# Self-attention scores on the two halves of the rows, with one unpadded copy of the turned keys

## The chip, the cores and the metric

The kernel runs on one core of a Trainium2 chip. The metric is the device time of one execution in microseconds (us), as the median of the runs made.

## The reference

One decoder layer over x of shape (4, 512, 256), in float32: causal linear self-attention with a quadratic feature map, cross-attention over a context of 1601 tokens, a mixture of eight experts (two for each token), each followed by a residual and a layer norm. The change lies in the self-attention:

```python
q = (x @ Wq.T)  # 16 heads of 16 features; k and v likewise
def feature_map(x):             # after a layer norm over the 16 features
    xn = norm(x) * gamma + beta
    diag, off = xn * xn, xn[..., IU] * xn[..., JU]
    return concat([diag * 16 ** -0.5, off * (2 / 16) ** 0.5])
kv_cum = cumsum(phi_k[..., :, None] * v[..., None, :], axis=time)
num = einsum('bhtf,bhtfd->bhtd', phi_q, kv_cum)
den = einsum('bhtf,bhtf->bht', phi_q, cumsum(phi_k)) + EPS
x = layernorm(x + (num / den) @ Wo.T)
```

The inner product of two such feature vectors is (q.k / 4) squared. The kernel therefore computes for each head the scores k.q, squares them, sets those of later keys to zero and multiplies them with the values and a column of ones.

## The kernel before

**Stages.** The opening loads and splits weights and prepares batch 0. Then comes the self-attention of four batches, then cross-attention, then the experts. Every engine runs its own program; semaphores order them.

**Numbers.** Float32 operands of a product are split into a high part in fp32r and the rest. A head has 16 features; q and k are laid out so that a head takes 64 rows (16 features in four slots: high, high, low, low for q and high, low, high, low for k in QX and KX), which makes the sum over 64 rows the sum over the four split products. Two heads fill the 128 rows.

**Quads and slots.** The 16 heads are taken in four quads of four (g), and the 512 keys in four blocks of 128 (c). A slot n is one quad and one block, n = 4g + c, 16 slots in a batch. In a slot the four heads j = 0 to 3 each have one score product (`score`, L1577; matmul L1584) of 128 keys against the queries from that block on: 512, 384, 256 or 128 columns for c = 0 to 3.

**Turned keys and queries.** `turn` on TensorE (L1562) transposes two heads at a time (q = 0, 1 within a quad) into bank 0 for the queries and bank 1 for the keys. ACT copies the queries whole into qT (L801): rows 0 to 63 hold the even head, rows 64 to 127 the odd one. DVE copies the keys in two casts of 64 rows (L1086, L1087) into kT, which has one plane of 128 rows for each of the four heads; the other 64 rows of each plane were set to zero by two memsets in the opening (L1027, L1028). So the score of a head contracts over all 128 rows, and the zeros cut the other head of the pair. TensorE may not turn the next keys before kT_ok says that bank 1 was read, and the first score of a quad waits for both turns.

**The order in a slot.** On TensorE (`attention`, L1641) slot n has: scores 0 and 1 of slot n + 1; the first half of the slot's other steps; scores 2 and 3; the four value products of slot n (`value`, L1594, 32 output rows for each head, with a different 32 columns of the array); the second half of the other steps. The scores use banks 3, 4 and 5 in turn, so a score waits until ACT has squared the third before it (`sqr_ok`, L1583). ACT squares (L836), POOL masks the diagonal block (L620), the values wait for the mask.

**The other steps** are written out in `alongside(n, b)` (L459). In slots 0 to 5 the batch before is finished (back, yt, out, stats); in slots 0 to 8 the next batch is projected and its features are made ("project qk" L1539, "project v" L1550, squares, variance, normalise L1073, affine on POOL L601 and L603); the turns of quad g + 1 stand at the end of quad g - 1 and the start of quad g, those of quad 3 in slots 7 and 8; slots 13 to 15 turn the first quads of the next batch. Slots 9 to 12 have hardly any such step on TensorE. On DVE the turns stand behind the features of the same slot. SP loads the turned input of the next batch but one once its buffer is free (L529), ACT splits it (L762), in slot 12 the one for two batches later.

Between the opening and the loop ACT issues nine copies that fill a DRAM buffer for the experts, XG, with numbers (L856, L859).

## Time and profile before

| | us |
|---|---|
| median of 3 runs | 1341.96 (1336.73 to 1345.72) |
| profiled execution | 1343.06 |
| its span, first to last instruction | 1341.3 |
| opening, ahead of the first score | 0 to 57 |
| self-attention loop | 57 to 282 |
| cross-attention and experts | about 300 to the end |

| over the span | busy us | share |
|---|---|---|
| TensorE, matmuls | 1188.4 | 89% |
| VectorE (DVE) | 745.2 | 56% |
| ScalarE (ACT) | 593.6 | 44% |
| GpSimd (POOL) | 700.1 | 52% |

All score products of the self-attention (L1584) take 76.5 us of matmul time, and the 64 casts of the turned keys (L1086, L1087) 43.9 us of DVE. Times in the trace count from the start of the span. A busy share of a matmul is no measure of its pace, since its end is modelled and successive ones overlap; the distance from one start to the next is.

### The profile page before, as it was taken

How to read it: one execution, taken by the hardware profiler on the slowest of the kernel's cores; microseconds unless marked ns; L12 is line 12 of the kernel's file. 1: busy time of each engine (PE TensorE's matmuls, PEld its weight loads, DVE VectorE, ACT ScalarE, POOL GpSimd, SP SyncE). 2: the span in 40 equal slices, each digit the busy share in tenths (PEclk: the TensorE clock that was granted, in tenths of full speed). 3: DMA queues.
4: the chain of work that ended last, by engine and by line, in shares of the span. 5: the costliest groups of instructions: out<-in, count | busy, mean ns of one | idle time of the engine just before them, and what ended most of it. 6: DMA issues, size and time to landing. Idle time of an engine off the chain costs nothing.

```text
span 1341.3 us, 19028 instructions
## 1 busy us (share of the span) xinstructions
PE 1188.4 (89%) x6456; PEld 696.4 (52%) x6456; DVE 745.2 (56%) x1364; ACT 593.6 (44%) x1033; POOL 700.1 (52%) x621
## 2 busy tenths in 40 slices
PE   4388898856999999999999999999999899999990
PEld 3254565533555545555555555555555356666660
DVE  5655857547236664555684467654657754433325
ACT  3366756632444464344644435643544423222222
POOL 1354737331358776577787577695777221311112
PEclk9599998886899999999999999999999999999995
DMA  5492000010000010000110000000001831211105
GB/s 170 148 327 90 2 1 1 1 50 26 0 0 1 1 50 1 1 1 0 35 32 17 1 1 1 25 32 1 1 1 62 281 115 44 76 42 39 45 24 188
DMA packets 33133, 64.84 MB, mean 48 GB/s; under 512 B 4349, under 2 KB 22526, under 8 KB 32768
## 3 DMA queue, kind: packets, MB, share of 16 engines
q1 hardware_dynamic: 23328, 32.41, 7.6%
q10 hardware_dynamic: 6304, 22.76, 5.4%
q0 software_dynamic: 3408, 8.46, 1.8%
q8 instruction: 54, 0.88, 0.3%
q14 instruction: 39, 0.32, 0.1%
HBM read 53.06 MB, written 28.51 MB: 61 GB/s over the span
## 4 chain that ended last, share of the span: by engine, by line
PE 71%; DVE 13%; issue 5%; ACT 5%; DMA 4%; ACTq 1%; POOL 1%; SPq 0%; POOLq 0%; DVEq 0%
PE PS L1772 15%; PE PS L1783 12%; PE PS L1675 10%; PE PS L1840 9%; DVE mxp L1405 5%; PE PS L1858 5%; DMA xt_raw<-in_xt 3%; PE PS L1688 3%; PE PS L1594 2%; PE PS L229 2%; PE PS L1573 2%; PE PS L1584 2%; PE PS L230 2%; PE PS L231 2%; PE PS L1849 1%
## 5 line engine op out<-in xcount | busy, mean ns | idle before, releaser
L682 POOL TENSOR_TENSOR acc<-acc,PX 128x1024 f32<-128x1024 f32 (+1 forms) x165 | 392.6, 2379 | 127.5 <-ACT PX L955 118.3
L955 ACT ACTIVATE PX<-PS 128x1024 f32<-128x1024 f32 (+1 forms) x208 | 212.3, 1025 | 257.7 <-PE PS L1772 254.5
L1405 DVE TENSOR_REDUCE mxp<-PS 128x2 f32<-128x804 f32 x256 | 242.1, 990 | 123.5 <-PE PS L1688 122.6
L1783 PE MATMUL PS<-PX,V 128*64 128x512 f32 (+1 forms) x832 | 207.8, 609 | 0.2 <-ACT PX L955 0.2
L1840 PE MATMUL PS<-W,XBT 128*128 x312 | 147.1, 595 | 1.1 <-ACT XBT L987 0.8
L731 POOL DMA_INDIRECT Y<-yb,goal_u x39 | 38.3, 982 | 202.5 <-DVE yb L1487 196.5
L620 POOL TENSOR_SCALAR_AFFINE_SELECT A<-A 128x128 f32<-128x128 f32 x256 | 85.8, 350 | 105.8 <-ACT A L836 103.0
L836 ACT ACTIVATE A<-PS 128x512 f32<-128x512 f32 (+3 forms) x256 | 97.1, 447 | 64.8 <-PE PS L1584 58.3
L1772 PE MATMUL PS<-QH,KH 64*128 64x512 f32 (+1 forms) x416 | 102.8, 491 | 3.4 <-ACT PX L955 2.7
L1772 PEld LDWEIGHTS PS<-QH,KH 64*128 64x128 f32 (+1 forms) x416 | 38.3, 181 | 116.0 <-issue 79.7
L1584 PE MATMUL PS<-qT,kT 128*128 128x512 f32 (+3 forms) x256 | 76.5, 376 | 15.9 <-ACT A L836 10.7
L1783 PEld LDWEIGHTS PS<-PX,V 128*64 128x64 f32 (+1 forms) x832 | 48.4, 136 | 78.0 <-issue 72.3
L1772 PE MATMUL PS<-QH,KL 64*128 64x512 f32 (+1 forms) x416 | 82.8, 393 | 0.0
L1772 PE MATMUL PS<-MR,one_row 64*128 64x512 f32 (+1 forms) x416 | 82.7, 392 | 0.0
L1772 PE MATMUL PS<-QL,KH 64*128 64x512 f32 (+1 forms) x416 | 82.5, 393 | 0.0
L1224 DVE RECIPROCAL TR<-TR 128x256 f32<-128x256 f32 x32 | 55.8, 1746 | 47.2 <-ACT TR L930 47.2
L1688 PE MATMUL PS<-KH,QH 64*128 64x402 f32 x512 | 72.5, 356 | 5.8 <-DVE mxp L1405 5.8
L1840 PEld LDWEIGHTS PS<-W,XBT 128*128 128x128 f32 x312 | 55.9, 191 | 41.8 <-issue 40.2
L1858 PE MATMUL PS<-W,hT 128*128 x312 | 73.9, 380 | 0.8 <-ACT hT L1000 0.8
L994 ACT ACTIVATE gl<-PS 128x512 f32<-128x512 f32 x39 | 23.3, 597 | 114.3 <-PE PS L1840 114.3
L924 ACT COPY V<-PS 128x512 f32<-128x512 f32 (+1 forms) x52 | 30.5, 586 | 96.8 <-PE PS L1675 96.8
L679 POOL TENSOR_TENSOR acc<-PX 128x1024 f32<-128x1024 f32 x15 | 35.5, 2367 | 65.1 <-ACT PX L955 65.0
(278 smaller groups left out, 2153.5 us busy)
## 6 DMA issues: line engine op xcount, KB each, us to landing
W<-in_w SPq DMA_DIRECT2D x24, 512.0 KB, 5.3
XB<-XG ACTq DMA_DIRECT2D x39, 130.0 KB, 2.1
yl<-Y SPq DMA_DIRECT2D x8, 512.0 KB, 6.8
X<-in_x SPq DMA_DIRECT2D x1, 2048.0 KB, 11.8
out<-X SPq DMA_DIRECT2D x8, 256.0 KB, 2.1
xt_raw<-in_xt SPq DMA_DIRECT2D x3, 512.0 KB, 4.3
c_raw<-in_ctxt SPq DMA_DIRECT2D x6, 200.0 KB, 2.5
c_raw<-in_ctxt SPq DMA_DIRECT2D x12, 100.0 KB, 2.6
```

The lines of the kernel that those rows point to most:

```text
L620: pool.affine_select(out=blk, in_=blk, compare_op=ALU.is_ge, fill=0.0, base=0, pattern=[[1, P]], channel_multiplier=-1).then_inc(mask_ok, 1)
L682: ins = pool.tensor_tensor(sums[0:r], sums[0:r], PX[0:r, (NL * p + t) % NP, :, :], ALU.add)
L836: act.activation(A[:, u % 8, P * c:T], PS[:, score_bank(b, u), P * c:T], ACT.Square, scale=0.25).then_inc(sqr_ok, 1)
L955: act.activation(PX[0:r, u % NP, :, :], PS[0:r, score_buffer(u):score_buffer(u) + 2, :], ACT.Exp, scale=XD ** -0.5)\
L1405: dve.tensor_reduce(mxp[:, p % 2, :, v % NT, v // NT:v // NT + 1].rearrange("p a o -> p (a o)"), PS[:, k:k + 2, 0:BW], AX, ALU.max)\
L1584: pe.matmul(PS[:, score_bank(b, u), P * c:T], kT[:, g % 2, j, P * c:P * c + P], qT[:, g % 2, j // 2, P * c:T], start=True, stop=True).then ...
L1675: mm = pe.matmul(o, l, r, start=(n == 0), stop=(n == len(ops) - 1))
L1688: mm = pe.matmul(bank(bk + half, BW), QH[rows, p % 2, P * i:P * i + P], KH[rows, p % 2, BSTART[k]:BSTART[k] + BW], start=True, stop=True)
L1772: mm = pe.matmul(bank(score_buffer(u) + half, rows=r), lhs, q_[rows, p % 2, :], start=(n == 0), stop=(n == 3))
L1783: mm = pe.matmul(PS[rows, 4, :], V[0:LROWS[j], j, P * p + XD * half:P * p + XD * half + XD], PX[0:LROWS[j], u % NP, half, :], start=(j == ...
L1840: mm = pe.matmul(bank(2 * m + j % 2), XBT[:, j % 2, c, :], W13[:, bass.ds(e, 1), m, c, :].rearrange("p o n -> p (o n)"), start=(c == 0), s ...
L1858: mm = pe.matmul(bank(6, D), hT[:, j % 2, f, :], W2[:, bass.ds(e, 1), f, :].rearrange("p o n -> p (o n)"), start=(f == 0), stop=(f == FC - 1))
```

## The change

The turned keys get the layout of the turned queries: kT shrinks from four planes to two, and one cast of 128 rows replaces two of 64 rows. The memsets go. Each score product contracts over the 64 rows that hold its head, rows 0 to 63 for heads 0 and 2 and rows 64 to 127 for heads 1 and 3, in kT as in qT. kT_ok counts one for each turn instead of two, const_dve one instead of three. The three banks of the scores, the order of the steps and all other waits stay as they are.

```diff
--- before.py
+++ after.py
@@ -97,7 +97,7 @@
         QX = ss("QX", [P, NT, SH, 4, SF], f32r)
         KX = ss("KX", [P, NT, SH, 4, SF], f32r)
         qT = ss("qT", [P, 2, 2, T], f32r)
-        kT = ss("kT", [P, 2, 4, T], f32r)
+        kT = ss("kT", [P, 2, 2, T], f32r)
         A = ss("A", [P, 8, T])
         VS = ss("VS", [P, NT, SH, 2 * SF])
         osb = ss("osb", [P, 2, T])
@@ -1024,8 +1024,6 @@
         @block.vector
         def _(dve):
             dve.memset(VS[:, :, :, SF:], 1.0).then_inc(const_dve, 1)
-            dve.memset(as32(kT[64:P, :, 0:4:2, :]), 0.0).then_inc(const_dve, 1)
-            dve.memset(as32(kT[0:64, :, 1:4:2, :]), 0.0).then_inc(const_dve, 1)
             groups = [raw[:, c, 0:2 * D].rearrange("p (g f) -> p g f", f=SF) for c in range(KC)]
             dve.wait_ge(ld_q, 16)
             for c in range(KC):
@@ -1083,8 +1081,7 @@
 
             def turn(b, g, q):
                 dve.wait_ge(tk_mm, 8 * b + 2 * g + q + 1)
-                dve.tensor_copy(kT[0:64, g % 2, 2 * q, :], bank(1, rows=64)).then_inc(kT_ok, 1)
-                dve.tensor_copy(kT[64:P, g % 2, 2 * q + 1, :], PS[64:P, 1, :]).then_inc(kT_ok, 1)
+                dve.tensor_copy(kT[:, g % 2, q, :], bank(1)).then_inc(kT_ok, 1)
 
             def quad_out(b, g):
                 dve.wait_ge(av_mm, 16 * b + 4 * g + 4)
@@ -1533,7 +1530,7 @@
         @block.tensor
         def _(pe):
             pe.wait_ge(const_pool, 3)
-            pe.wait_ge(const_dve, 3)
+            pe.wait_ge(const_dve, 1)
             pe.wait_ge(w_lo, 1)
 
             def project_qk(t, i):
@@ -1576,13 +1573,14 @@
 
             def score(b, n, j):
                 g, c, u = n // NT, n % NT, 4 * n + j
+                rows = slice(64 * (j % 2), 64 * (j % 2) + 64)
                 if c == 0 and j == 0:
                     pe.wait_ge(qT_ok, 8 * b + 2 * g + 2)
-                    pe.wait_ge(kT_ok, 16 * b + 4 * g + 4)
+                    pe.wait_ge(kT_ok, 8 * b + 2 * g + 2)
                 if started(b, u, 3):
                     pe.wait_ge(sqr_ok, 64 * b + u - 2)
-                pe.matmul(PS[:, score_bank(b, u), P * c:T], kT[:, g % 2, j, P * c:P * c + P],
-                          qT[:, g % 2, j // 2, P * c:T], start=True, stop=True).then_inc(sc_mm, 1)
+                pe.matmul(PS[:, score_bank(b, u), P * c:T], kT[rows, g % 2, j // 2, P * c:P * c + P],
+                          qT[rows, g % 2, j // 2, P * c:T], start=True, stop=True).then_inc(sc_mm, 1)
 
             def value(b, n, j):
                 g, c, u = n // NT, n % NT, 4 * n + j
@@ -1615,7 +1613,7 @@
                 if kind == "turn q":
                     turn(b, s[1], s[2], QX, 0, tq_mm, qT_ok, 1)
                 if kind == "turn k":
-                    turn(b, s[1], s[2], KX, 1, tk_mm, kT_ok, 2)
+                    turn(b, s[1], s[2], KX, 1, tk_mm, kT_ok, 1)
                 if kind == "back":
                     back(b, i)
                 if kind == "yt":
```

## Rows read from the trace of the kernel before

**Rows 1.** Windows, all engines: window, length, busy (xcount) by engine, PEclk, DMA share, GB/s.

```profile
110.00:170.00 60.00, 50.42 (x350) 31.94 (x348) 42.65 (x91) 41.02 (x104) 33.87 (x73) 0.97 0.03 10
```

**Rows 2.** Chain (start, length, what), then timeline: start, us, engine, line, xcount [idle <-releaser].

```profile
65.86 44.31 DMA xt_raw<-in_xt
...
110.19 1.04 ACT L762 CAST xt_h<-xt_raw 128x1024 fp32r<-128x1024 f32 x1 [1.66 <-DMA xt_raw<-in_xt]
```

**Rows 3.** Tiles osb and kT: ns min/median/max, starts, forms; what readers waited for.

```profile
L1093 DVE COPY osb<-PS x16: 679/692/693, 77.6 to 282.8; 128x512 f32<-128x512 f32 x16
...
L1087 DVE CAST kT<-PS x32: 694/694/695, 52.7 to 270.5; 64x512 fp32r<-64x512 f32 x32
...
  ACT A L836: 35.6, 51
```

**Rows 4.** Timeline of the opening, and one DMA issue (KB, us to landing).

```profile
0.79 0.45 SPq L511 DMA_DIRECT2D raw<-in_wqkv  x1
...
4.71 1.76 DVE L1028 MEMSET kT<- 64x2048 f32 x1 [0.48 <-issue]
6.48 1.28 DVE L1032 TENSOR_REDUCE w_mean<-raw 128x32 f32<-128x512 f32 x2
...
53.50 1.09 PE L1573 MATMUL PS<-ident,KX 128*128 128x128 f32 x4 [0.64 <-DVE kT L1087]
...
raw<-in_wqkv SPq DMA_DIRECT2D x1, 768.0 KB, 5.7
```

**Rows 5.** Timeline at the start of batch 1's scores.

```profile
116.48 0.69 DVE L1087 CAST kT<-PS 64x512 fp32r<-64x512 f32 x1
...
117.28 0.70 PE L1584 MATMUL PS<-qT,kT 128*128 128x512 f32 x2 [1.55 <-issue]
```

**Rows 6.** Timeline of DVE, POOL, PE, slots 8 to 12 of batch 1.

```profile
156.03 0.69 DVE L1087 CAST kT<-PS 64x512 fp32r<-64x512 f32 x1
...
162.49 1.64 POOL L601 TENSOR_TENSOR feat<-feat,gam 128x512 f32<-128x512 f32 x1 [1.32 <-DVE feat L1073]
...
166.33 3.33 PE L1594 MATMUL PS<-A,VS 128*32 128x512 f32 x8 [1.94 <-POOL A L620]
```

**Rows 7.** Chain in batch 3: start, length, what.

```profile
268.31 0.71 DVE kT L1087
```

**Rows 8.** Timeline of PE in cross-attention, where shapes change.

```profile
576.48 0.40 PE L1772 MATMUL PS<-QH,KL 64*128 64x512 f32 x2
576.71 0.40 PE L1772 MATMUL PS<-MR,one_row 64*128 64x512 f32 x2
577.04 0.50 PE L229 MATMUL PS<-x_h,WQh 128*128 128x512 f32 x1
577.38 0.40 PE L230 MATMUL PS<-x_l,WQh 128*128 128x512 f32 x1
577.61 0.39 PE L231 MATMUL PS<-x_h,WQl 128*128 128x512 f32 x1
...
644.14 0.28 PE L230 MATMUL PS<-WOl,OHL 128*128 128x256 f32 x1
644.26 0.28 PE L231 MATMUL PS<-WOh,OHL 128*128 128x256 f32 x1
644.47 0.50 PE L1772 MATMUL PS<-QH,KH 64*128 64x512 f32 x2
644.81 0.39 PE L1772 MATMUL PS<-QL,KH 64*128 64x512 f32 x2
```

**Rows 9.** Timeline of PE in self-attention: scores before a projection.

```profile
135.25 0.60 PE L1584 MATMUL PS<-qT,kT 128*128 128x384 f32 x2
135.69 0.28 PE L229 MATMUL PS<-WSh,y_h 128*128 128x256 f32 x1
...
140.91 0.39 PE L1584 MATMUL PS<-qT,kT 128*128 128x256 f32 x2
141.14 0.28 PE L229 MATMUL PS<-WSh,y_h 128*128 128x256 f32 x1
```

## What the change will do to the time

> **What bounds the kernel now.** I read the busy time by stage first. In the self-attention stage no engine is full: of 60 us the TensorE records hold 50.4, DVE 42.7, ACT 41.0, POOL 33.9, at a granted clock of 0.97 [rows 1]. So the chain of work, not a busy share, has to say what an edit is worth. The change touches nothing but this stage (57 to 282 us) and the opening ahead of it.
>
> The chain shows a pin. The load of the third batch's turned input is issued at 65.86 us behind the copies that fill XG and lands at 110.17, 44.31 us later; ACT stands still for it 1.66 us (L762) [rows 2]. Whatever the score loop gains before 110 us in batch 0 is therefore waited away, except a gain in the opening, which starts the copies themselves earlier. So I count the opening, the last slots of batch 0 and batches 1 to 3.
>
> From there to 282 us a batch has two halves. In slots 0 to 8 and 13 to 15 TensorE has projections, transposes and output products between the scores and is nearly back to back; in slots 9 to 12 it has almost only scores and values and waits for squares (ACT), masks (POOL) and, through POOL's affine step, for DVE.
>
> **Part 1: the copies and memsets on DVE.** The 32 pairs of casts into kT (0.69 us each) become 32 casts of 128x512 [rows 3]. The nearest row for such a copy out of PSUM, osb of 128x512, takes 0.69 us as well [rows 3], so each turn loses 0.70 us, 22 us of DVE time in all. Where is it on the path?
>
> - Opening: the transposes of the second k turn wait for the L1087 cast (start 53.50, idle 0.64 for it) [rows 4], and the q turn behind them is what ACT copies before it issues the XG copies. 0.7 us, which moves the pin too.
> - The two memsets end at 4.71 + 1.76 = 6.47 us and the first reduce starts at 6.48; but the qkv weights, issued at 0.79 us, need 5.7 us, so they land at 6.5 anyway [rows 4]. Nothing; at most the 0.5 us that separates DVE instructions there. Without the DMA's cover it would be some 4 us.
> - Start of a batch: TensorE idles 1.55 us before its scores at 117.28, until the L1087 cast of 116.48 is done [rows 5]. The pattern stands three times (batches 1, 2, 3), all other engines idle too: 3 x 0.7 = 2.1 us.
> - Slots 7 to 11: DVE runs without a gap over two turns (the last cast at 156.03), the layer norm and the features; POOL waits 1.32 us for it at 162.49, then does its two affine steps (the first takes 1.64) and the masks, and the values at 166.33 have waited 1.94 us for a mask [rows 6]. Two casts less (1.4 us) put this about 1.3 us earlier, just what POOL idled; ACT's squares are late next. In batches 1 and 2: 2.7 us. In batch 0 the pin takes it, batch 3 has no features.
> - Batch 3: one turn has its cast on the chain at 268.31, the transposes behind it start at its end [rows 7]: 0.7 us.
>
> Sum of part 1: 0.7 + 2.1 + 2.7 + 0.7 = 6.2 us gained. The lower end is 2.8 (opening and batch starts alone, if another engine takes over elsewhere), the upper 7.
>
> **Part 2: the scores on half the rows.** A 512-column matmul over 128 rows takes 0.23 us from start to start (577.38 to 577.61), and a pair over 64 rows each, one per half, takes the same 0.23 (576.48 to 576.71) [rows 8]. So scores 0 and 1, and 2 and 3, of a slot can share one stream: per pair 0.23, 0.175, 0.12 and at most 0.09 us saved at 512, 384, 256 and 128 columns (from 0.23 for two of 256 [rows 9]).
>
> Against that stands the change of shape. In cross-attention the last pair of 64 rows before a 128-row product takes 0.33 instead of 0.23 (576.71 to 577.04) and that product 0.34 instead of 0.23; the other way 0.21 instead of 0.12 (644.26 to 644.47) and 0.34 instead of 0.23 [rows 8]. One boundary between the two shapes costs 0.20 us. Today scores and projections have one shape: two scores of 256 columns go straight into a projection in 0.23 [rows 9]. Where transposes stand ahead, 0.09 is paid already (0.44 for two of 384, not 0.35 [rows 9]), so such a boundary adds 0.11. The boundary between scores and values (128x32) exists now and stays. Afterwards a slot with other work reads: work, boundary, pair, boundary, work, boundary, pair, values. Three new boundaries for two pairs.
>
> The ledger of a full batch, what is paid minus what is saved, in us: slot 0: 0.42 - 0.35; 1: 0.51 - 0.24; 2: 0.20 - 0.05 (the rest lies under a wait for y_l); 3: nothing, since ACT's copy and squares time it; 4: 0.42 - 0.35; 5: 0.60 - 0.24; 6: 0.60 - 0.10; 7: 0.11 - 0.23; 8: 0.11 - 0.18; 9 to 12: nothing, since two shapes alternate now too and ACT and POOL time them; 13: 0.31 - 0.24; 14: 0.42 - 0.10; 15: 0.31 - 0.34. Together 4.0 paid and 2.4 saved, 1.6 us lost. Batches 1 and 2: 3.2. Slots 13 to 15 of batch 0: 1.0 - 0.7 = 0.3. Batch 3, which has fewer steps: 2.2 - 1.6 = 0.6. Sum of part 2: 11.2 paid, 7.1 saved, 4.1 us lost.
>
> The three banks are in both kernels: the fourth score of a slot waits for the first square, and scores idled 35.6 us for squares in all [rows 3]. This is why slots 3 and 9 to 12 give nothing: a score that starts sooner waits longer for ACT. The waits before a score are as before; kT_ok only counts half.
>
> The rows put a price of 0.20 us on a change of shape. The Trainium skill, TensorEngine Tiling (Array Packing), Key Properties, says that changing the tiling mode drains TensorE, which speaks against mixing 64-row scores into 128-row work; the trace agrees (0.20 us a boundary) and the sum goes by the trace. The same page, Theoretical Speedup, gives up to 2x for 64 rows; by that alone part 2 would be the gain of the first rival below.
>
> **Sum.** 4.1 - 6.2 = -2.1 us. The profiled execution took 1343.06 us with a span of 1341.3, so 1.8 lie around it; changed it would take 1341.0. It lies 1.1 us above the median 1341.96, so the forecast for the median is 1340.0, a change of 0.15%, which a comparison will hardly show.
>
> **Rivals.**
> 1. Shape changes cost nothing here, because each score waits for its own semaphore anyway. Then 7.1 + 6.2 = 13.3 us are gained: 1328.7. For it: pairs do run together in cross-attention. Against it: each boundary in rows 8 is paid, without exception. Chance 0.1.
> 2. Slower: the pairs don't overlap, because here each matmul has its own wait and its own increment where cross-attention increments once after a row of them. The boundaries remain: 11.2 - 6.2 = +5.0, so 1347.0. It decides for slower as soon as less than 5 of the 7.1 us are saved (6.2 + saving < 11.2). By the same mechanism 1% slower needs boundaries of 0.35 us. The drain that the page names is this rival's other half. Chance 0.2.
> 3. The DVE casts give only the lower 2.8 us, because ACT takes over in slots 8 to 12. Then 4.1 - 2.8 = +1.3: 1343.3. Chance 0.15.
> 4. Nothing in slots changes because the clock moves: TensorE falls to a lower granted clock after idle stretches, and a shifted idle stretch moves a few us either way. I give it 0.05 with no time of its own.
> The forecast has 0.5.
>
> **How the numbers follow.** The likeliest case is 1340, by itself 1335 to 1345 (half the boundaries' price either way, 2 us, and the spread of the runs shown, 1336.7 to 1345.7). The range reaches up to rival 2 with some spread, 1349, and down most of the way to rival 1, 1331. What a measurement of this kernel can tell from no change is about 1%, 13.4 us: faster means under 1328.5, slower over 1355.4. Only part of rival 1 gets under the first (0.05), and rival 2 with dearer boundaries over the second (0.04).
>
> **What would show it.** Right: one cast of about 0.69 us in each k turn; the idle before the first scores of batches 1 to 3 at 0.85 instead of 1.55 us; the 1.32 us that POOL waits for the features gone or ACT's; two scores of 256 columns in 0.12 to 0.2 us, and a 64-row pair ahead of a projection followed by a gap of 0.1 on either side; the stage's end (the last scores, now at 281 us) near 279; the load of the third input landing near 109.5. Wrong: pairs whose starts lie a full stream apart (rival 2), projections right behind scores with no gap (rival 1), an end of the stage over 285 or under 272, or times after it that differ in length, which would be no work of this change.

## The result, and the profile after

The changed kernel took 1353.34 us in the median of five runs (1349.41 to 1354.15), against 1344.75 us for the kernel before in runs beside it. The ratio is 1.0067, with an interval of 1.0045 to 1.009. Twelve more runs of it later gave 1351.56 us and 1.0051 (1.003 to 1.0071). So the change costs 7 to 9 us. I had forecast a gain of 2.

The profiled execution took 1352.12 us with a span of 1350.4. From its page come the sums by engine, the granted clock in 40 slices, and the group of the scores (busy us, mean ns, idle before them and what ended it); the last line is the clock of the kernel before:

```profile
PE 1202.1 (89%) x6456; PEld 685.6 (51%) x6456; DVE 717.2 (53%) x1330; ACT 594.6 (44%) x1033; POOL 700.0 (52%) x621
...
PEclk9599899876899999999999999999999999999995
...
L1582 PE MATMUL PS<-qT,kT 64*128 64x512 f32 (+3 forms) x256 | 64.1, 440 | 14.3 <-ACT A L836 11.7
...
PEclk9599998886899999999999999999999999999995
```

DVE is down by 28.0 us (745.2 to 717.2), of which the copies into kT are 21.9 and the memsets 3.5, and the score products by 12.4 us (76.5 to 64.1). Yet TensorE as a whole is busy 13.7 us *longer*. That can't be the scores; other products of the stage became longer. The clock slices are where to look: the fifth (135 to 169 us) and the ninth (270 to 304) are lower than before, the seventh is higher.

The last row of value products of the self-attention starts at 286.78 us, where it was at 281.41 before. A second profile of the changed kernel has it at 285.06. Behind that row the changed kernel needs another 1063.6 and 1061.8 us, the one before 1059.9, with the same instructions; so 2 to 4 us of the loss appear behind the stage.

### Where the changed kernel did what I said

The tile kT: ns min/median/max, first and last start, shapes.

```profile
L1582 PE MATMUL PS<-qT,kT x256: 276/436/794, 53.9 to 286.4; 64*128 64x512 f32 x32, 64*128 64x384 f32 x32, 64*128 64x256 f32 x32, 64*128 64x128 f32 x32
...
L1084 DVE CAST kT<-PS x32: 678/691/692, 50.6 to 271.9; 128x512 fp32r<-128x512 f32 x32
```

One cast of 0.691 us stands where two of 0.69 stood [rows 3]. The slowest score took 794 ns, though; I come back to it. The timeline of the changed kernel shows the opening, the start of batch 1, and then TensorE at two places where scores stand among other work (start, us, engine, line, xcount, idle before and its releaser):

```profile
6.77 1.28 DVE L1030 TENSOR_REDUCE w_mean<-raw 128x32 f32<-128x512 f32 x2 [4.79 <-DMA raw<-in_wqkv]
...
117.36 0.50 PE L1582 MATMUL PS<-qT,kT 64*128 64x512 f32 x2 [0.83 <-ACT qT L801]
...
120.76 0.60 PE L1570 MATMUL PS<-ident,QX 128*128 128x128 f32 x4
121.29 0.45 PE L1582 MATMUL PS<-qT,kT 64*128 64x384 f32 x2
121.66 1.07 PE L1592 MATMUL PS<-A,VS 128*32 128x512 f32 x8
...
141.41 0.40 PE L231 MATMUL PS<-WSh,xt_l 128*128 128x512 f32 x1
141.74 0.38 PE L1582 MATMUL PS<-qT,kT 64*128 64x256 f32 x2
142.05 0.39 PE L229 MATMUL PS<-WSh,y_h 128*128 128x256 f32 x1
142.27 0.28 PE L230 MATMUL PS<-WSl,y_h 128*128 128x256 f32 x1
```

- The memsets were worth nothing: without them the first reduce waits 4.79 us for the weights and starts at 6.77 (6.48 before [rows 4]).
- TensorE idles 0.83 us before the first scores of a batch, where it was 1.55 [rows 5]; the same number stands at 177.93 and at 237.01. The step said 0.85.
- A pair of 256-column scores between two projections: 0.33 from the projection to the pair, 0.31 for the pair, 0.22 for the next product, together 0.86 us. With 128 rows the three distances are 0.23, 0.23 and 0.12 [rows 8, 9], 0.58 in all. The pair costs 0.28 more; the ledger had 0.40 - 0.12 = 0.28.
- Behind four transposes the pair starts after 0.53 us. In the kernel before the like distance is 0.35, so a boundary behind transposes costs 0.18, not the 0.11 of the ledger.

### Where it did not

TensorE at the end of slot 8 and in slot 9 of batch 1, in the changed kernel:

```profile
152.19 0.44 PE L1582 MATMUL PS<-qT,kT 64*128 64x384 f32 x2
154.05 0.66 PE L1570 MATMUL PS<-ident,QX 128*128 128x128 f32 x4 [1.42 <-ACT qT L801]
154.63 0.44 PE L1582 MATMUL PS<-qT,kT 64*128 64x384 f32 x2
155.00 1.58 PE L1592 MATMUL PS<-A,VS 128*32 128x512 f32 x8
156.52 1.12 PE L1570 MATMUL PS<-ident,KX 128*128 128x128 f32 x4
```

and at the same place in a kernel with part 1 alone (casts only, e1 below):

```profile
149.76 0.60 PE L1581 MATMUL PS<-qT,kT 128*128 128x384 f32 x2
151.57 0.66 PE L1570 MATMUL PS<-ident,QX 128*128 128x128 f32 x4 [1.21 <-ACT qT L801]
151.98 0.60 PE L1581 MATMUL PS<-qT,kT 128*128 128x384 f32 x2
152.51 1.07 PE L1591 MATMUL PS<-A,VS 128*32 128x512 f32 x8
153.50 0.66 PE L1570 MATMUL PS<-ident,KX 128*128 128x128 f32 x4
```

In both, TensorE has finished its pair and stands still until ACT has copied the turned queries: 1.42 us here, 1.21 there. Behind it the same eight value products take 1.58 us here and 1.07 there, the same four transposes 1.12 and 0.66. That is not another amount of work; the granted clock is 0.50 from 156 to 172 us here and 1.00 there, that is the level of 1.2 GHz in place of 2.4.

The idle stretch is 0.2 us longer here, but that doesn't decide it. A kernel of the experiments below, e14, has the instructions of the changed one up to this place and waits just as long:

```profile
153.38 0.66 PE L1570 MATMUL PS<-ident,QX 128*128 128x128 f32 x4 [1.43 <-ACT qT L801]
153.97 0.45 PE L1582 MATMUL PS<-qT,kT 64*128 64x384 f32 x2
154.34 1.07 PE L1592 MATMUL PS<-A,VS 128*32 128x512 f32 x8
```

Its clock stays at 1.00 for another 10 us. And e3, also below, waits only 1.02 us at this place and is at 0.50 right behind it. So the same instructions meet either level, and the length of the wait doesn't tell which.

The windows give the table by stage. I cut each batch where it can be recognised in any kernel: at its first score, and, in batches 1 and 3, where TensorE waits for the turned queries of slot 8 or stands before its thin slots. Columns: window, length, busy (xcount) of PE, PEld, DVE, ACT, POOL, then the granted clock, DMA share, GB/s. Changed:

```profile
117.40:154.00 36.60, 33.47 (x238) 21.22 (x238) 17.80 (x46) 23.16 (x60) 16.53 (x41) 1.00 0.01 1
154.00:177.90 23.90, 21.94 (x114) 10.01 (x115) 17.10 (x37) 17.29 (x44) 16.49 (x33) 0.64 0.00 1
177.90:237.00 59.10, 52.03 (x352) 29.83 (x353) 35.00 (x81) 39.38 (x102) 33.12 (x73) 0.97 0.00 1
237.00:260.50 23.50, 19.93 (x154) 11.83 (x155) 8.84 (x15) 15.44 (x38) 9.42 (x30) 1.00 0.01 1
260.50:289.30 28.80, 25.77 (x142) 11.38 (x142) 12.50 (x30) 15.98 (x39) 12.19 (x35) 0.64 0.20 58
```

Casts only (e1):

```profile
116.30:151.60 35.30, 32.25 (x239) 23.13 (x239) 18.06 (x46) 23.13 (x60) 16.69 (x41) 1.00 0.01 1
151.60:173.60 22.00, 18.36 (x115) 9.48 (x115) 18.32 (x37) 17.00 (x44) 17.46 (x33) 1.00 0.00 1
173.60:232.10 58.50, 51.84 (x353) 33.28 (x353) 35.16 (x81) 39.20 (x102) 33.35 (x73) 0.94 0.01 1
232.10:254.30 22.20, 19.14 (x154) 13.18 (x155) 8.85 (x15) 15.40 (x38) 9.40 (x30) 1.00 0.00 1
254.30:277.60 23.30, 19.83 (x142) 10.99 (x142) 12.48 (x30) 15.86 (x39) 12.11 (x35) 0.93 0.17 48
```

Row by row the counts of instructions agree to one or two, and DVE, ACT and POOL are busy for nearly the same time. The stretches differ by 1.3, 1.9, 0.6, 1.3 and 5.5 us. Where both clocks are 1.00 the difference is 1.3 (first and fourth row). The two rows with 0.64 in the changed kernel hold 7.4 of the 10.6 us. That they do doesn't yet say that the clock is the reason.

### The profile page after: what moved, and what is told of

Read it like the earlier page. It is cut to its first block, busy times and chain, and to the rows that moved or that the text cites. A ratio compares the mean times of both kernels' runs of the same rounds, so it can differ in the third digit from the quotient of the medians.

```text
span 1350.4 us, 18994 instructions
## 1 busy us (share of the span) xinstructions
PE 1202.1 (89%) x6456; PEld 685.6 (51%) x6456; DVE 717.2 (53%) x1330; ACT 594.6 (44%) x1033; POOL 700.0 (52%) x621
## 4 chain that ended last, share of the span: by engine, by line
PE 75%; DVE 13%; ACT 5%; issue 4%; DMA 2%; ACTq 1%; POOL 0%; SPq 0%; POOLq 0%; DVEq 0%
PE PS L1770 15%; PE PS L1781 12%; PE PS L1673 10%; PE PS L1838 9%; DVE mxp L1402 5%; PE PS L1856 5%; PE PS L1592 4%; PE PS L1582 3%; PE PS L1686 3%; PE PS L1570 3%; PE PS L229 3%; PE PS L230 2%; PE PS L231 2%; PE PS L1847 1%; PE PS L1751 1%
## 5 line engine op out<-in xcount | busy, mean ns | idle before, releaser
L1582 PE MATMUL PS<-qT,kT 64*128 64x512 f32 (+3 forms) x256 | 64.1, 440 | 14.3 <-ACT A L836 11.7
## 6 DMA issues: line engine op xcount, KB each, us to landing
out<-X SPq DMA_DIRECT2D x8, 256.0 KB, 2.1
```

The source lines that it names most:

```text
L1582: pe.matmul(PS[:, score_bank(b, u), P * c:T], kT[rows, g % 2, j // 2, P * c:P * c + P], qT[rows, g % 2, j // 2, P * c:T], start=True, stop ...
```

## The experiments

One number recurs below: **the time at the lower clock**. I took the granted clock in windows of 2 us and added 2 x (1 - clock) x 2 us, so that a window at 0.50 counts whole. "Stage" is the distance from the first score to the last row of value products in the profile, "behind" the distance from there to the end of the span. The lower clock is given from 50 to 310 us, as the expectations have it, and for the stage and what is behind it. The first of the three misleads: in a kernel with a longer stage it holds less of the 18 to 30 us at the lower clock that stand in the 30 us or so behind the stage in every kernel. So I go by the other two. The ratio is to the kernel before, run beside it, with its 95% interval.

| kernel | median us | ratio | last value at | stage | behind | at lower clock, 50 to 310 | in the stage | behind it |
|---|---|---|---|---|---|---|---|---|
| before | 1344.75 | | 281.41 | 224.6 | 1059.9 | 55 | 31 | 76 |
| changed | 1353.34 | 1.0067 (1.0045–1.009) | 286.78 | 232.9 | 1063.6 | 72 | 56 | 84 |
| e11, changed again | 1351.56 | 1.0051 (1.003–1.0071) | 285.06 | 231.1 | 1061.8 | 69 | 48 | 86 |
| e1, casts only | 1338.26 | 0.9975 (0.9958–0.9992) | 275.42 | 220.5 | 1062.9 | 48 | 17 | 87 |
| e12, casts only again | 1342.14 | 0.9974 (0.9958–0.9991) | 272.97 | 219.4 | 1060.2 | 42 | 14 | 76 |
| e2, 64 rows only | 1364.29 | 1.017 (1.0143–1.0198) | 291.94 | 237.6 | 1066.8 | 79 | 60 | 108 |
| e3, no pairs | 1376.08 | 1.025 (1.0222–1.0279) | 309.64 | 256.0 | 1065.0 | 96 | 93 | 99 |
| e4, changed, filled | 1359.38 | 1.0145 (1.0107–1.0182) | 284.62 | 231.1 | 1064.5 | 52 | 31 | 96 |
| e5, before, filled | 1345.85 | 1.0013 (0.9994–1.0032) | 281.01 | 224.0 | 1059.9 | 45 | 21 | 75 |
| e6, changed, steps last | 1372.33 | 1.0182 (1.0136–1.0229) | 307.64 | 254.0 | 1065.8 | 83 | 78 | 100 |
| e7, before, steps last | 1352.57 | 1.0081 (1.0051–1.0111) | 289.81 | 235.6 | 1059.4 | 35 | 24 | 76 |
| e8, 64 rows in slots 9, 11, 12 | 1346.35 | 1.0022 (1.0001–1.0043) | 281.31 | 224.5 | 1065.4 | 62 | 31 | 102 |
| e9, boundaries added to e1 | 1369.01 | 1.0171 (1.0143–1.0199) | 303.00 | 247.9 | 1064.8 | 31 | 27 | 92 |
| e10, half of them | 1349.99 | 1.0031 (1.0013–1.0049) | 284.34 | 229.4 | 1060.0 | 38 | 20 | 76 |
| e13, 128 rows in slots 9 to 12 | 1356.65 | 1.0033 (1.0011–1.0055) | 282.43 | 228.8 | 1072.8 | 52 | 34 | 98 |
| e14, 128 rows in batch 3 | 1353.74 | 1.0000 (0.9988–1.0012) | 282.96 | 229.2 | 1071.1 | 65 | 48 | 97 |
| e15, 64 rows in slots 9, 11, 12 | 1350.97 | 0.998 (0.9962–0.9997) | 275.23 | 222.1 | 1071.1 | 55 | 31 | 97 |

e13 to e15 ran later, when the kernel before took 1353.9 us, and what is behind the stage took some 10 us longer; of these only the ratios and the stages compare with the others. e1, e9, e10, e12 to e15 don't compute the reference: where a score takes in all 128 rows without the zeros, it adds the other head of the pair. The work is that of right scores.

### e1, e2, e3: the parts alone, and the pairs taken apart

**e1** is the changed kernel with the scores over all 128 rows again.

```diff
-                rows = slice(64 * (j % 2), 64 * (j % 2) + 64)
-  ... kT[rows, g % 2, j // 2, P * c:P * c + P], qT[rows, g % 2, j // 2, P * c:T]
+  ... kT[:, g % 2, j // 2, P * c:P * c + P], qT[:, g % 2, j // 2, P * c:T]
```

> Part 1 alone: the changed kernel with kT in two planes, one cast for each turn and no memsets, but each score contracts over all 128 rows again. Without zeros it adds the other head of the pair to each score, so the numbers differ; the work on every engine is that of the kernel before less the casts and memsets. If the loss comes from the change of shape on TensorE (my theory), this kernel keeps the gain of part 1 alone and takes about 6 us less than the kernel before (1338 to 1340 beside 1344.8). If the rival is right, that the lost 9 us come from the casts (DVE free earlier, PE and ACT colliding differently), this kernel is as slow as the changed one, about 1353.

Measured: 0.9975, some 3.4 us faster than before. The stage ends 6.0 us earlier in this profile and 8.4 in that of e12, where I had said 6.2. Some 2 to 3 us of the 6.0 and 8.4 are the first score, which stands later in the profile before; the stage itself is 4.1 and 5.2 us shorter, near the 5.5 that I had said behind the opening. In the time 3.4 us are left (the interval allows 1 to 6), in both sets of runs. The larger miss lies in part 2, which costs 11.4 us (286.78 - 275.42) and 12.1 us (285.06 - 272.97) at the last value.

**e2** is the kernel before, its four planes and two casts kept, with the 64-row slices in the score.

```diff
+                rows = slice(64 * (j % 2), 64 * (j % 2) + 64)
-  ... kT[:, g % 2, j, P * c:P * c + P], qT[:, g % 2, j // 2, P * c:T]
+  ... kT[rows, g % 2, j, P * c:P * c + P], qT[rows, g % 2, j // 2, P * c:T]
```

> Part 2 alone: the kernel before (two casts, four planes, memsets) with scores over the 64 rows that hold the head. Shape theory: the whole loss and no gain of the casts, so 6 us slower than the changed kernel and 12 to 16 slower than before (1357 to 1361 beside 1344.8), and the clock windows between 150 and 290 us as low as in the changed kernel. Rival (the two parts only cost together): within 3 us of the kernel before.

Measured: 1.017, 22 us slower than before, more than the 12 to 16 expected and twice what the same slices cost on top of the casts (10 to 12 us by the ratios 1.0067 to 0.9975 and 1.0051 to 0.9974). Do the two parts not add up, then? In the stage they do. e2 takes 13.0 us longer there than the kernel before, and the same slices on top of the casts 12.4 and 11.7 us (232.9 - 220.5, 231.1 - 219.4). The excess stands behind the stage, where the instructions are the same: 1066.8 us against 1059.9, with 108 us at the lower clock against 76. Why the clock is lower there in e2 no run shows.

**e3** takes the heads in the order 0, 2, 1, 3, so that two successive scores lie on the same half of the rows. Work and boundaries are those of the changed kernel; only the overlap is gone.

```diff
+                h = (0, 2, 1, 3)[j]
+                rows = slice(64 * (h % 2), 64 * (h % 2) + 64)
   (and h in place of j where value picks its head)
```

> The changed kernel with the heads of a quad taken in the order 0, 2, 1, 3 in scores and values: neighbouring scores then lie on the same half of the rows and can't run at once, while the shapes, boundaries and sizes are as in the changed kernel. If pairs of scores really overlap there (starts of a pair nearly together), this takes 5 to 8 us more than the changed kernel (the 7 us of the ledger). If their own waits and increments keep them apart anyway, it takes the same time.

Measured: 1.025. A pair of 256 columns takes 0.44 us from its start to the next instruction (0.31 in the changed kernel):

```profile
128.29 0.50 PE L1583 MATMUL PS<-qT,kT 64*128 64x256 f32 x2
128.73 0.66 PE L1626 MATMUL PS<-ident,y 128*128 128x128 f32 x4
```

So the pairs do overlap in the changed kernel, and that is worth some 25 us of the run (1.025 less 1.0067, of 1342), where I expected 5 to 8. Rival 2's mechanism is out. What 64 rows cost before that saving is 37 us (1.025 less 0.9975). My ledger had 11.2 paid and 7.1 saved: both are over three times as large in the run, and their difference, 4.1 in the ledger, is 10 to 12. e3 also has 93 us at the lower clock in its stage, where casts only has 14 and 17.

At full clock the ledger nonetheless holds. From the first score of batch 1 to the wait of slot 8, with a granted clock of 1.00 in all three, e1 takes 35.24 us, the changed kernel 36.69 and e3 38.52. Paid: 3.28 (38.52 - 35.24), in the ledger 3.17 (slot 15 and slots 0 to 8, without the boundary behind the wait). Saved: 1.83 (38.52 - 36.69), in the ledger 1.90.

### e4 and e5: TensorE kept busy in the thin slots

Two spare products of 512 columns, behind a wait for the squares of the next batch, between scores and values in slots 8 to 12, in the changed kernel (**e4**) and in the one before (**e5**). They write a bank that nobody reads then.

```diff
+                    if n in (8, 9, 10, 11, 12):
+                        pe.wait_ge(sq_ok, NT * (b + 2 if more else b + 1))
+                        for _ in range(2):
+                            pe.matmul(bank(2), WSh[:, 0, 0:P], WSh[:, 0, 0:2 * D], start=True, stop=True)
```

> The changed kernel with two extra 512-column products in each of slots 8 to 12, between the scores and the values, from weights into bank 2, which nothing reads: more work, on TensorE alone, in the stretch where its clock falls to half. If the lower clock there is a consequence of TensorE's emptier stretches and costs time, the granted clock of 154 to 173 us and 276 to 290 us goes back to full and the kernel gets 3 to 8 us faster than the changed one. If the boundaries alone explain the loss, it gets 0 to 5 us slower (20 slots x 2 x 0.23 = 9 us of work, half of it in waits).

> The kernel before with two extra 512-column products in each of slots 8 to 12, as in the filled variant of the changed kernel. If more work on TensorE keeps its clock up there, the granted clock of 164 to 180, 224 to 231 and 258 to 265 us stays full and it is as fast as the kernel before or up to 4 us faster. If the work only adds up, 2 to 10 us slower.

In e4's profile the clock stays up in the stretch where the changed kernel lost it:

```profile
154.00:173.00 19.00, 17.38 (x112) 7.79 (x104) 15.38 (x29) 14.33 (x39) 15.64 (x28) 0.91 0.00 1
```

against, in the changed kernel,

```profile
154.00:173.00 19.00, 17.84 (x82) 7.67 (x83) 14.87 (x32) 14.18 (x34) 14.84 (x27) 0.55 0.00 0
```

112 products against 82 in the same 19 us, some of them the spare ones. But that profile is the fastest of e4's runs (1350.85 us). They reach up to 1369.15, and by the ratios the kernel is 10 to 13 us *slower* than the changed one (1.0145 against 1.0067 and 1.0051). The test is inconclusive: the clock came back in the one profile, the time did not, and e14 shows that the clock can stay up here without any filling. In the kernel before, the same products cost nothing (1.0013), so they lie in idle time there. The clock is up in one of the places that I had named (224 to 231 us, 1.00 in place of 0.54) and as before in another (164 to 180 us, 0.79 both), and nothing is gained.

### e6 and e7: fewer boundaries

If the boundaries around the inner pair are the cost, then putting all four scores of a slot together should take away two of them. The steps of a slot go behind the values.

```diff
-                        if j == 1:
-                            for d, s in steps[:half]:
-                                step(b + d, s)
...
-                    for d, s in steps[half:]:
+                    for d, s in steps:
```

> The changed kernel with another order on TensorE alone: the four scores stand together and all other steps of the slot follow the values, so a slot has three boundaries between shapes (work to scores, scores to values, values to work) instead of up to five. Boundary theory: 2 boundaries x 0.2 us x some 40 slots with work in the middle, up to 16 us at full clock, come back less what the fourth score now waits for its bank: 4 to 12 us faster than the changed kernel (1342 to 1350). Rival (boundaries are cheap, the loss is the clock alone, by emptier stretches): TensorE now waits more between scores, the clock falls longer, and it is slower than the changed kernel by 3 us or more.

> The control for the order: the kernel before with the same order (four scores, values, then all other steps). It has two boundaries in a slot either way, so no boundary is saved; only the wait of the fourth score for its bank, no longer covered by work, is new. Boundary theory: 2 to 8 us slower than the kernel before, so the gap between the 64-row and the 128-row scores in this order (this kernel against the one above) is smaller than in the old order, under 6 us with the casts' gain counted. Rival: this order helps or hurts both kernels alike.

This fell. By the ratios e6 is 15 to 18 us slower than the changed kernel, and e7 11 us slower than before (expected: 4 to 12 faster, and 2 to 8 slower); their distance is 14 us (20 by the medians), more than the 7 to 9 between the kernels they come from. The timeline of e6 shows why: the fourth score now follows the third at once and stands there until ACT has squared.

```profile
124.94 0.44 PE L1582 MATMUL PS<-qT,kT 64*128 64x384 f32 x1 [0.40 <-ACT A L836]
...
133.62 0.32 PE L1582 MATMUL PS<-qT,kT 64*128 64x128 f32 x1 [0.77 <-ACT A L836]
```

From 60 to 300 us the scores' products wait 36.7 us for ACT (62 times), in the changed kernel 11.7 (14); in e7 it is 30.3 (57), in the kernel before 10.7 (15). The steps between the pairs are what hides ACT's squares behind three banks, in both kernels. The time at the lower clock in the stage is 78 us in e6 and 24 in e7, which waits nearly as much: waiting alone doesn't bring the clock down, and 64 rows make the difference here too.

### e8: 64-row scores only where TensorE has little else

The kernel before, with the scores of slots 9, 11 and 12 (issued in the slot ahead) on 64 rows.

```diff
+                rows = slice(64 * (j % 2), 64 * (j % 2) + 64) if n in (10, 12, 13) else slice(0, P)
```

> The kernel before (four planes, two casts) with 64-row pairs only for the scores issued in slots 9, 11 and 12 of each batch, where no other step stands between scores and values, so that no boundary is added. By the ledger these slots give nothing: the same time as the kernel before within 2 us, and the granted clock of 155 to 175 us as before. If it is the pairs themselves that let the clock fall (less work for the same scores), the clock falls in these slots as it does in the changed kernel and it is 3 to 8 us slower than the kernel before.

Measured: 1.0022, no gain. The stage takes 224.5 us (224.6 before) with the same 31 us at the lower clock, and the clock in 154 to 173 us is 0.91, as before. So 64-row pairs in those slots neither cost nor bring the lower clock there. What the profile has more than the one before stands behind the stage (1065.4 us).

### e9 and e10, with e11 and e12: boundaries without pairs

Do the gaps at the boundaries bring the lower clock? e1 keeps 128-row scores; **e9** adds, ahead of scores 0 and 2 of every slot, a 64-row product of four columns into the same bank, which the score then overwrites. **e10** adds it ahead of score 0 alone. The changed kernel and the casts alone ran again beside them (e11, e12).

```diff
+                if j in (0, 2):        # e10: (0,)
+                    pe.matmul(PS[:, score_bank(b, u), P * c:P * c + 4], kT[0:64, g % 2, j // 2, P * c:P * c + P],
+                              qT[0:64, g % 2, j // 2, P * c:P * c + 4], start=True, stop=True)
```

> The casts-only kernel (scores over all 128 rows, contents differ by the other head) with a product of 64 rows and 4 columns put ahead of scores 0 and 2 of every slot, into the start of the bank that the score then overwrites: four added boundaries in a slot (the changed kernel has three), next to no added stream, and the scores stay full height. Theory A, the gaps at the boundaries let the clock fall: time at half clock between 50 and 310 us rises from 48 to 70 or more as in the two kernels with 64-row scores, and the time is 20 to 40 us over the casts-only kernel (1338). Theory B, the clock falls because scores of half the rows count as less work: half-clock time stays at 45 to 55 us, and the time is only the boundaries' price over the casts-only kernel, 10 to 18 us.

> The same with the small product ahead of score 0 alone: two added boundaries in a slot. A price for each boundary that is constant gives half of what the run above adds (theory B: 5 to 9 us over the casts-only kernel; theory A: 10 to 20). If clock falls set in at some point, the second pair of boundaries costs much more than the first.

> The changed kernel once more, for a second profile on the same chip as the casts-only kernel: 9 to 15 us over that one. If the low clock in slots 8 to 15 of batches 1 and 3 belongs to the kernel, the second profile shows 65 us or more at half clock between 50 and 310 us again; if it was chance, some 50 us, as in the profile of the kernel before.

> The casts-only kernel once more, for a second profile: 3 to 6 us under the kernel before, and some 45 to 55 us at half clock between 50 and 310 us. If half-clock time scatters by 20 us from profile to profile of one kernel, it can't be put down to the change.

The timeline of e9: the small product takes 0.17 us from its start to that of the scores.

```profile
120.11 0.24 PE L1582 MATMUL PS<-qT,kT 64*128 64x4 f32 x1 [0.83 <-ACT qT L801]
120.28 0.73 PE L1584 MATMUL PS<-qT,kT 128*128 128x512 f32 x2
120.84 0.60 PE L1570 MATMUL PS<-ident,QX 128*128 128x128 f32 x4
```

Measured: e9 costs 26.9 us over e12 (128 such products, 0.21 us each), e10 7.9 us (64, 0.12 each; 23 of these stand behind values, where a change of shape exists already, 24 behind transposes). e9's time lies in theory A's range, e10's in theory B's. And the clock? By the count from 50 to 310 us e9 has the least time at the lower level of all kernels here, 31 us. But its stage ends at 303 us, and what follows a stage at the lower clock falls out of that count. The windows of the whole stage, of e9, of the changed kernel and of casts only (e12):

```profile
55.09:303.00 247.91, 227.58 (x1414) 143.08 (x1413) 119.79 (x267) 151.43 (x382) 119.52 (x281) 0.94 0.23 77
```

```profile
53.89:286.78 232.89, 202.81 (x1285) 110.46 (x1284) 119.31 (x267) 150.48 (x381) 120.94 (x281) 0.88 0.25 84
```

```profile
53.56:272.97 219.41, 187.07 (x1287) 118.27 (x1285) 120.95 (x266) 149.66 (x382) 122.21 (x280) 0.97 0.26 86
```

In the stage e9 has 27 us at the lower clock, casts only 14 and 17, the changed kernel 56 and 48. So the added boundaries bring 10 to 14 us of it at most, though e9 has more of them than the changed kernel; the rest, some 25 us, goes with the 64-row scores themselves. It is not their being shorter: in e3 a pair takes 0.44 us against 0.23 with 128 rows, and the lower clock is most of all. Of e9's 27 us the clock can hold only a few; boundaries have a price of their own, above what I expected.

The repeats show how firm this is: e11 falls to the lower level at the same places as the changed kernel (154 to 172, 260 to 271, 280 to 298 us), e12, like e1, keeps 1.00 behind the wait of slot 8 (148 to 164 us) and has a short stretch at 0.61 only from 164 to 168.

e12 also answers for POOL. I had said that its wait of 1.32 us for the features [rows 6] would go or become ACT's. It is shorter, 1.07 us, and still there:

```profile
160.02 1.65 POOL L601 TENSOR_TENSOR feat<-feat,gam 128x512 f32<-128x512 f32 x1 [1.07 <-DVE feat L1071]
```

Measured from the batch's first score, this instruction starts 0.7 us earlier than before (44.55 against 45.2), not 1.3.

### e13, e14, e15: where do the 64 rows cost?

The changed kernel with 128-row scores in some places.

```diff
-                rows = slice(64 * (j % 2), 64 * (j % 2) + 64)
+                rows = slice(0, P) if COND else slice(64 * (j % 2), 64 * (j % 2) + 64)
# e13: COND = n in (10, 11, 12, 13)   e14: b == B - 1   e15: n not in (10, 12, 13)
```

> The changed kernel with scores over all 128 rows (contents differ by the other head) only where they are issued in slots 9 to 12; no boundary is saved but those in slot 10. Clock theory: slots 9 to 12 keep full clock, half-clock time between 50 and 310 us falls from 70 to 45 to 55, and it is 4 to 8 us faster than the changed kernel (1352). If the low clock follows from what comes before these slots (the 64-row scores in slots 0 to 8), nothing changes: 1350 to 1353.

> The changed kernel with scores over all 128 rows in batch 3 alone (contents differ by the other head there). The second half of batch 3 took 28.8 us in the changed kernel and 23.3 in the casts-only one, the first half 23.5 and 22.2. So batch 3 alone should give back 6 to 7 us: 1345 to 1346 beside 1352, with full clock from 262 to 275 us and the last value near 279. If the clock there carries over from batch 2, only the 1.3 us of the first half come back.

> The changed kernel with scores over all 128 rows (contents differ by the other head) everywhere but in slots 9, 11 and 12, where 64-row pairs add no boundary. Boundary theory: all added boundaries are gone, so it takes the casts-only time, 1338 to 1343; the clock in those slots decides the last 3 us. If 64-row scores in exactly these slots are what lets the clock fall, it lies midway, 1346 to 1349, with 60 us or more at half clock.

**e14** gives batch 3 its 128 rows back and returns to the time of the kernel before: 1.0000, that is 7 to 9 us less than the changed kernel (0.0051 and 0.0067 of 1350), where I expected 6 to 7. Its batch 3 takes 43.96 us from first score to last value, the changed kernel's 49.8 and 48.4, casts only 43.3 and 42.9. The two halves of it in e14:

```profile
239.00:261.20 22.20, 19.15 (x154) 13.18 (x155) 8.84 (x15) 15.41 (x38) 9.43 (x30) 0.99 0.01 1
...
261.20:285.20 24.00, 21.21 (x143) 11.92 (x143) 12.60 (x30) 15.91 (x39) 12.12 (x35) 0.87 0.16 46
```

The first equals casts only (22.20), the second lies 4.8 us under the changed kernel's 28.80. Work at full clock can hold about 1 us of it (the first halves differ by 1.3); the rest goes with 0.87 in place of 0.64. The clock did fall behind the quiet stretch at 260 us here too, but it was back at 268.

**e15** keeps 64 rows only in slots 9, 11 and 12 and has the ratio of casts only (0.998 and 0.9975). What the change cost lies outside these slots, or needs the rest of the slots as well. **e13**, 128 rows in slots 9 to 12, leaves nearly all added boundaries in place and gives back 2 to 5 us by the ratio, with 34 us at the lower clock in the stage in place of 56 and 48; I had said 4 to 8. Its second half of batch 3 takes 25.2 us at 0.86.

## Why the prediction was wrong, step by step

Batches, in us from first score to first score (the last to its last value), means of the two profiles of either kernel:

| | changed | casts only | difference | my ledger |
|---|---|---|---|---|
| batch 0 | 62.5 | 61.7 | 0.8 | 0.3 |
| batch 1 | 61.3 | 57.6 | 3.7 | 1.6 |
| batch 2 | 59.1 | 57.6 | 1.5 | 1.6 |
| batch 3 | 49.1 | 43.1 | 6.0 | 0.6 |

**What bounds the kernel, the pin.** Half wrong, without weight. The load of the third input is issued at 63.68 us, and when ACT comes to L762 at 109.61 it doesn't wait. The loop itself arrives there, so batch 0 was not free. It cost 0.8 where I counted 0.3, by profiles of the changed kernel that differ by 1.9 there.

**Part 1, sum 6.2 us.** About right in the stage (4.1 and 5.2 of the 5.5 behind the opening), high for the time: 3.4, near the 2.8 of rival 3. That is 3 of the 9 to 11 us by which the forecast missed. Part of it is batch 0, which takes 61.4 and 61.9 us with casts only and 60.4 before. The batch starts came as written (0.83). The memsets were worth nothing, as written. Slots 7 to 11 gave less on POOL than I said (0.7 of 1.3 us a batch). The opening can't be read: the first score stands at 56.86 before, at 56.85 and 57.03 in e8 and e5, but at 54.37 and 54.24 in e2 and e7, all with both casts; with one cast it stands at 53.12 to 55.09. So the profiles scatter there by more than 0.7.

**Part 2, the ledger at full clock.** Right, 1.45 measured for 1.3 where the clock is 1.00 (36.69 - 35.24), and 0.28 for 0.28 on the single pair. One term was too small, the boundary behind transposes: 0.18 for 0.11. The Trainium skill, TensorEngine Tiling (Array Packing), Key Properties, says that changing the tiling mode drains TensorE, and the trace agrees, with 0.28 us net around a pair. The speedup of up to 2x that the Trainium skill gives there under Theoretical Speedup is seen only inside the pair (0.31 against 0.44 us in e3).

**The step that failed: pricing everything at full clock, "9 to 12: nothing" first of all.** The end of the stage, 286.78 us, is past the 285 that I had named as a sign of being wrong. I wrote that these slots cost nothing, since ACT and POOL time them. That would be so at an even clock. In fact the stage with 64-row scores has 48 to 56 us at the lower clock where casts only has 14 to 17. In slots 8 to 15 of batch 1 the granted clock is 0.64 (154 to 178 us) where casts only has 1.00; the stretch is 1.9 us longer. In batch 3 it is 5.5 us. Eight value products of 512 columns take 1.58 us (slot 8) and 1.93 (batch 3) in place of 1.07, and a 512-column score up to 0.79. The clock had no term in the ledger. Batch 3 is worst; there TensorE has the fewest steps between the scores, but that this is why I have not shown. In 4-us windows of the changed kernel,

```profile
257.00:261.00 4.00, 1.42 (x14) 0.60 (x6) 2.45 (x5) 1.86 (x5) 1.92 (x4) 1.00 0.00 0
261.00:265.00 4.00, 4.00 (x24) 1.80 (x26) 2.05 (x11) 1.55 (x5) 2.15 (x5) 0.53 0.00 0
265.00:269.00 4.00, 3.65 (x20) 2.09 (x20) 2.52 (x3) 3.26 (x6) 1.26 (x4) 0.50 0.00 0
269.00:273.00 4.00, 3.64 (x19) 1.27 (x17) 1.06 (x3) 2.10 (x6) 0.82 (x3) 0.69 0.00 0
```

and of casts only:

```profile
252.00:256.00 4.00, 1.69 (x14) 0.89 (x14) 3.52 (x11) 1.09 (x5) 1.90 (x4) 0.87 0.00 0
256.00:260.00 4.00, 4.00 (x26) 2.77 (x22) 1.61 (x5) 2.51 (x5) 2.10 (x5) 0.71 0.00 0
260.00:264.00 4.00, 2.94 (x22) 1.66 (x21) 2.06 (x3) 3.32 (x8) 1.35 (x5) 1.00 0.00 0
```

Both kernels lose the clock behind the same quiet stretch. Casts only has it back at 260 us, the changed kernel only around 271, and then loses it again at 278.

**A size for it.** The best measure stands behind the stage, where all kernels have the same instructions. In the fourteen profiles before e13 that part takes 1059.4 to 1066.8 us, and it is ordered by its time at the lower clock: 75 to 76 us of it go with 1059.4 to 1060.2 us, 84 to 87 with 1061.8 to 1063.6, 92 to 108 with 1064.5 to 1066.8. A straight line through them gives 0.22 us for each us at the lower clock. The single runs of one kernel say the same: in four sets of 17 to 29 runs of the kernel before, the time rises by 0.24 to 0.28 us for each us at the lower clock (worked out from each run's granted clock and span). By these rates the 35 to 39 us that the changed kernel has more than casts only in the stage are worth 8 to 11 of the 12 us. With the 4.1 of my ledger for the boundaries that makes 12 to 15. So the larger part of the miss goes with the clock, and the ledger of part 2 needs no other large term for the changed kernel. This is an estimate; a split by stretches doesn't come out even, as the next table shows.

The changed kernel, e11 and e14 (of the later runs) have the same instructions up to batch 3. Length in us, with the time at the lower clock in brackets:

| | changed | e11 | e14 |
|---|---|---|---|
| batch 0 | 63.5 (17) | 61.5 (10) | 61.5 (10) |
| batch 1, to the wait of slot 8 | 36.7 (0) | 38.2 (3) | 38.2 (3) |
| batch 1, the rest | 23.9 (17) | 23.9 (17) | 25.1 (10) |
| batch 2 | 59.1 (3) | 59.1 (3) | 60.6 (17) |

In three of the four rows more time at the lower clock goes with a longer stretch. In the third, which is mostly the thin slots, it doesn't: there "ACT and POOL time them" may have been right, and the 1.9 us of that stretch may have another cause.

**The rivals.** Rival 2's time (1347.0) was the nearest and its mechanism wrong, as e3 shows: pairs overlap. Rival 4 named what moved, the clock, but I gave it neither a direction nor a time, although the kernel before has the lower clock already (31 us of it in the stage, and 0.87 from 259.5 to 283.6 us). A price for a microsecond at the lower level could have been had from like instructions at either level. The direction could not: that kernel has no 64-row scores in the stage, and the length of the waits doesn't tell it (e3 and e14 above).

**After the stage.** I had named times that differ behind it as a sign that something else is at work. They do differ, by up to 7 us, and go with the clock as said. The changed kernel has 2 to 4 us of its loss there. No run shows whether the change has a part in that.

**What stays open.** 64-row scores next to other work go with more time at the lower clock in the stage: 48 to 93 us in the changed kernel, e2, e3, e6 and e14, and 31 and 34 in e4 and e13, against 14 to 31 in the kernels with 128 rows (e8 and e15, with few pairs, have 31). That time at the lower clock costs 0.2 to 0.3 us for each is read from profiles and runs that happen to differ in it; e4, which was meant to set the clock by itself, came out slower. What exactly makes the clock fall or return, no run here separates, nor why it is lower behind the stage in e2, e8 and others.

## What to carry to other kernels

Packing two heads onto the halves of the array pays inside the pair (0.13 us here for 256 columns) and is paid for at each change of shape (0.18 to 0.20 us). Count the boundaries before the savings: pack where many products of one shape stand in a row, not two at a time between work of the full height. And before calling a slot free because TensorE waits there for another engine, look at the granted clock around it: a ledger at full clock has no term for it. When you count time at the lower clock, count it over the same instructions in each kernel, not over the same microseconds. No kernel here that computes the reference was faster than the one before. The single cast by itself was worth 3.4 us and would need another way to keep the heads apart.

## What I had not expected of the hardware

- 12.4 us fewer in the scores' busy time came with 13.7 us more on TensorE as a whole, because other products ran at the lower clock.
- The same instructions behind the same wait (1.42 and 1.43 us) ran at 0.50 in one profile and at 1.00 for another 10 us in the other.
- 128 added products of four columns with their changes of shape cost 26.9 us, most of it not by the clock (27 us at the lower level in the stage, 14 and 17 without them).
- Boundary costs and overlap gains were each over three times the ledger's sums in whole runs (37 and 25 us for 11.2 and 7.1). Part of that is the lower clock (93 us of it in e3's stage); that a late score also makes ACT's square late, and with it the score three banks on, I have only argued.
